# Normalising, transposing and splitting the next step's x inside the current one, and expert tiles by transposing DMAs

## The reference

```
h  = layernorm(x);  v = h@Wv+bv;  q = elu(h@Wq+bq)+1;  k = elu(h@Wk+bk)+1     # 16 heads of 16
s_t = s_(t-1) + k_t v_t^T;  z_t = z_(t-1) + k_t                               # per batch and head
x1 = x + (q_t s_t / (q_t z_t + 1e-6)) @ Wo + bo
h2 = layernorm(x1);  logits = h2 @ router_w^T;  the 2 largest of 8, softmax over them
out = x1 + sum over the 2 experts of prob * (gelu(h2 @ w1^T + b1) @ w2^T + b2)   # 256 -> 512 -> 256
```

## Time and profile before

| | us |
|---|---|
| median of 3 runs (1094.77 to 1099.10) | 1096.58 |
| profiled execution | 1091.56 |
| its span, first to last instruction | 1089.8 |
| TensorE busy | 951.3 (87%) |
| VectorE busy | 831.0 (76%) |
| ScalarE busy | 660.6 (61%) |
| GpSimd busy | 699.4 (64%) |
| xg load, issue to landing (median) | 3.0 |
| store of x1 (out<-x), issue to landing (median) | 3.2 |

### The profile page before, as it was taken

One profiled execution on the slowest core, in us unless ns is written; L12 is line 12 of the kernel. 1 busy time (PEld: TensorE's weight loads), 2 busy tenths in 40 slices (PEclk: granted clock), 3 DMA queues, 4 the chain that ended last, 5 costly groups with the idle time before them and its releaser, 6 DMA issues. The chain is left out here.

```text
span 1089.8 us, 33554 instructions
## 1 busy us (share of the span) xinstructions
PE 951.3 (87%) x10092; PEld 784.3 (72%) x10093; DVE 831.0 (76%) x2201; ACT 660.6 (61%) x1253; POOL 699.4 (64%) x606
## 2 busy tenths in 40 slices
PE   4599888988898898888889833999999999999995
PEld 2377667766766775675677733999999999999994
DVE  5378999998997997997999874666666666666663
ACT  5667776776776677666767432555555555555552
POOL 5626677786677678776778553556556565566555
PEclk9799999999998999998999966999999999999998
DMA  3665886446654654673655282455555555555554
GB/s 111 149 142 125 274 178 156 126 153 161 165 126 137 159 132 135 155 173 98 164 139 139 89 316 97 89 90 96 96 96 88 87 98 96 97 85 95 92 97 49
DMA packets 129125, 140.30 MB, mean 129 GB/s; under 512 B 12512, under 2 KB 122208, under 8 KB 128416
## 3 DMA queue, kind: packets, MB, share of 16 engines
q1 hardware_dynamic: 101184, 102.38, 38.0%
q0 software_dynamic: 26688, 35.93, 17.8%
q10 hardware_dynamic: 1184, 1.18, 0.3%
HBM read 72.01 MB, written 67.44 MB: 128 GB/s over the span
## 5 line engine op out<-in xcount | busy, mean ns | idle before, releaser
L1497 POOL DMA_INDIRECT out<-yt,to_token x142 | 225.7, 1589 | 172.8 <-DVE yt L1360 108.6
L792 ACT ACTIVATE ahl<-pS 128x512 f16<-128x512 f32 x240 | 141.0, 599 | 74.7 <-PE pS L508 73.1
L1035 DVE SCALAR_TENSOR_TENSOR ahl<-pS,ahl 128x512 f16<-128x512 f32 x240 | 161.2, 682 | 28.8 <-ACT ahl L792 27.5
L1414 POOL DMA_INDIRECT expert_in<-xn,cur x128 | 130.5, 1020 | 35.1 <-issue 33.1
L960 ACT ACTIVATE g<-pS,b1s 128x256 f32<-128x256 f32 x144 | 60.2, 470 | 90.7 <-PE pS L433 90.7
L433 PE MATMUL pF<-xT,was 128*128 128x512 f16 x384 | 102.7, 410 | 11.8 <-DVE xT L1040 11.8
L505 PE MATMUL pS<-cbs 128*128 128x512 bf16 x240 | 93.0, 387 | 20.2 <-DVE ahl L1035 12.2
L1331 DVE TENSOR_TENSOR ghl<-g,ghl 128x1024 f16<-128x1024 f32 x71 | 87.1, 1227 | 24.3 <-ACT ghl L982 24.3
L433 PE MATMUL pU<-w2s,ghl 128*128 x864 | 100.5, 273 | 1.9 <-DVE ghl L1331 1.9
L433 PE MATMUL pS<-gT,w1s 128*128 128x256 f16 x864 | 101.1, 274 | 0.1
L433 PE MATMUL pF<-w2s,ghl 128*128 x840 | 97.4, 273 | 0.0
(11 more groups left out here) (160 smaller groups left out, 2323.9 us busy)
## 6 DMA issues: line engine op xcount, KB each, us to landing
xg<-expert_in SPq DMA_DIRECT2D x71, 260.0 KB, 3.0
qk_parts<-qkhl SPq DMA_DIRECT2D x32, 512.0 KB, 2.9
qst<-qk_parts SPq DMA_DIRECT2D x96, 128.0 KB
kst<-qk_parts SPq DMA_DIRECT2D x48, 256.0 KB
xs<-x SPq DMA_DIRECT2D x16, 512.0 KB, 4.6
xr<-x SPq DMA_DIRECT2D x16, 512.0 KB, 4.8
out<-x SPq DMA_DIRECT2D x16, 512.0 KB, 3.2
expert_in<-pads SPq DMA_DIRECT2D x16, 260.0 KB, 3.7
```

What stands on the lines that cost most here:

```text
L792: nc.scalar.activation(ahl[:, b % 2, 0, n * 4 * C:(n + 1) * 4 * C], score_bank(fr, n)[:], ACT.Relu).then_inc(sc_hi, 1)
L1035: V.scalar_tensor_tensor(ahl[:, b % 2, 1, cols], score_bank(fr, n)[:], 0.0, ahl[:, b % 2, 0, cols], ALU.max, ALU.subtract).then_inc(sc_lo, 1)
L1414: G.indirect_dma_start(xg_dram, bass.IndirectOffsetOnAxis(ap=cur[:, qp, 2 * b + t:2 * b + t + 1], axis=0), xn2[:, qp, b], None).then_inc(s ...
L1497: G.indirect_dma_start(out, bass.IndirectOffsetOnAxis(ap=to_token[:, c % 2, s:s + 1], axis=0), yt[:, c % 2, s], None, compute_op=ALU.add). ...
```

## The change

1. x of step i+1: its statistics, moments and shift come early in body c, `normalise(i+1)` after the row copies' start, `x_transposes(i+1)`, `x_hi` and `x_lo` in the last third of body c. Only body 0 has them at its start, for step 0. Step 2's stand in the back-only body of step 1.
2. The order of work in a body is new on TensorE, ScalarE, VectorE and GpSimd: among others `out_transpose(r, 3)` comes after `project(1)`, `values(0)` and `values(1)` earlier, `v_low` before the third state update.
3. `norm2_apply` writes over x1 in place, after the store of x1 to the output has landed; TensorE transposes for the router from x1. New are `rows_high` (ScalarE, two per step) and `rows_low` (VectorE, two per step), which write the row as 256 f16 high parts and 256 f16 low parts in the same 1 KB that held 256 floats.
4. An expert tile comes by one DMA that transposes 256 rows x 512 f16 from DRAM into gT (128 partitions x 4 blocks x 256), and one small one for the last four floats of each row (about). There are four buffers of each in place of two; `turn`, the expert stage's `rows_high` and the low part by VectorE are gone. The loops of tiles have four tiles per turn in place of two.

```diff
+BUFS = 4
-        xn2 = sb("xn2", [P, 2, B, ROW], F32, att)
+        data = sb("data", [P, 2, B, ROW], F32, att)
-        xg = sb("xg", [P, 2, 2, ROW], F32, moe)
-        gT = sb("gT", [P, 2, 2, KC * MT], F16, moe)
+        about = sb("about", [P, BUFS, 2, ROW - D], F32, moe)
+        gT = sb("gT", [P, BUFS, 2, KC, MT], F16, moe)
+        rows = data[:].bitcast(F16)
...
@@ SP, expert tiles
-                if c >= 2:
-                    sp.wait_ge(gt_ps, t - 1)
-                    sp.wait_ge(meta, t - 1)
-                sp.dma_start(xg[:, c % 2], xg_dram[bass.ds(row, MT), :].rearrange("(s p) d -> p s d", p=P)).then_inc(xg_in[c % 2], 16)
+                if c >= BUFS or not isinstance(j, int):
+                    sp.wait_ge(h_ps, 2 * t - 2 * BUFS + 2)
+                    carry_wait(sp)
+                    sp.wait_ge(meta, t - BUFS + 1)
+                    carry_wait(sp)
+                sp.dma_start_transpose(gT[:, c % BUFS].rearrange("p a k n -> p (a k) n"),
+                                       xg_dram[bass.ds(row, MT), 0:D].bitcast(F16)).then_inc(gT_in[c % BUFS], 16)
+                sp.dma_start(about[:, c % BUFS],
+                             xg_dram[bass.ds(row, MT), D:ROW].rearrange("(s p) d -> p s d", p=P)).then_inc(about_in[c % BUFS], 16)
...
@@ TensorE, a body
-                if fr:
-                    x_transposes(0)
-                    x_transposes(1)
+                if c == 0:
+                    x_transposes(0, 0)
+                    x_transposes(0, 1)
                 if bk:
                     scores(0, 0)
-                if ro:
-                    out_transpose(r, 3)
+                if fr:
+                    project(0)
                 if bk:
                     scores(0, 1)
                 if turn_k:
                     k_rows(0)
+                if fr:
+                    project(1)
+                if ro:
+                    out_transpose(r, 3)
                 if sc:
                     route_positions()
...
-                if fr:
-                    project(0)
                 if bk:
                     scores(0, 2)
+                if turn_k:
+                    k_rows(1)
+                if fr:
+                    project(2)
                 if ro:
                     out_project(r, 3)
-                if fr:
-                    project(1)
                 if bk:
                     scores(0, 3)
-                if turn_k:
-                    k_rows(1)
-                if bk:
                     scores(1, 0)
-                if fr:
-                    project(2)
-                if bk:
                     attend(0)
+                if fr:
+                    project(3)
+                if bk:
                     scores(1, 1)
...
+                if turn_next:
+                    x_transposes(i + 1, 0)
                 if bk:
                     scores(2, 3)
                     out_project(s, 1)
+                if turn_next:
+                    x_transposes(i + 1, 1)
...
@@ TensorE, an expert tile
-                    pe.wait_ge(gt_lo, t + 2)
+                    pe.wait_ge(gT_in[p4], 16 * ((c + 1) // BUFS + 1) + 16 * j)
...
                 if is_tile(j, c + 1):
                     hidden_layer()
-                if is_tile(j, c + 2):
-                    turn()
                 if is_tile(j, c):
                     second_layer()
...
@@ ScalarE
+                def rows_high(n):
+                    act.wait_ge(xn2_done, 4 * r + 2 * n + 2)
+                    if c >= 4 and n == 0:
+                        act.wait_ge(scat_out[c % 2], 128 * rh)
+                    nc.scalar.activation(rows[:, c % 2, 2 * n:2 * n + 2, 0:D], x1[:, 2 * n:2 * n + 2], ACT.Copy).then_inc(rows_hi, 1)
...
                 if bk:
                     score_hi(0, 0)
-                if ro:
-                    out_hi(r, 3)
+                if fr:
+                    feature_in(0)
                 if bk:
                     score_hi(0, 1)
                 if turn_k:
                     kn_rows(0)
+                if fr:
+                    feature_exp(0)
+                    feature_in(1)
+                if ro:
+                    out_hi(r, 3)
...
                 if ro:
+                    rows_high(0)
                     row_copy(0)
+                    rows_high(1)
+                if turn_next:
+                    normalise(i + 1, 0)
                 if bk:
                     score_hi(2, 0)
                 if ro:
                     row_copy(1)
                 if fr:
                     qk_high(3)
+                if turn_next:
+                    normalise(i + 1, 1)
...
@@ VectorE
                 def norm2_apply(b):
                     if b == 0:
                         dve.wait_ge(ln2_rs, r + 1)
+                        dve.wait_ge(x1_out, 16 * r + 16)
-                    V.scalar_tensor_tensor(xn2[:, rp, b, 0:D], x1[:, b], mv2[:, b, 0:1], rs2[:, b:b + 1].to_broadcast([P, D]),
+                    V.scalar_tensor_tensor(x1[:, b], x1[:, b], mv2[:, b, 0:1], rs2[:, b:b + 1].to_broadcast([P, D]),
                                            ALU.subtract, ALU.mult).then_inc(xn2_done, 1)
+                def rows_low(n):
+                    dve.wait_ge(rows_hi, 2 * r + n + 1)
+                    V.scalar_tensor_tensor(rows[:, rp, 2 * n:2 * n + 2, D:2 * D], x1[:, 2 * n:2 * n + 2], 1.0,
+                                           rows[:, rp, 2 * n:2 * n + 2, 0:D], ALU.mult, ALU.subtract).then_inc(rows_lo, 1)
...
                 if bk:
                     score_lo(0, 0)
+                    score_lo(0, 1)
                 if ro:
                     out_lo(r, 3)
-                    residual(r, 2, c % 2)
-                if bk:
-                    score_lo(0, 1)
+                    residual(r, 2, c % 2, c == 2)
+                if turn_next:
+                    norm1_stats(i + 1)
                 if sc and c != STEPS:
                     row_data()
...
@@ GpSimd
                 if fr:
                     feature(0)
+                    feature(1)
+                    low(0)
                 if ro:
                     rstd(r, ve2, rs2, ln2_ve, ln2_rs)
-                if fr:
-                    feature(1)
-                    low(0)
+                if nx and c >= 2 or c == 1 and not front:
+                    rstd(i + 1, ve1, rs1, ln1_ve, ln1_rs)
+                if fr:
                     feature(2)
                     low(1)
```

More of the change, by code:

```diff
@@ L632, in body @@
                 if bk:
+                    scores(1, 1)
                     out_transpose(s, 0)
@@ L1213, in body @@
                         score_lo(1, 3)
+                    if ro:
+                        rows_low(0)
+                if fr:
+                    values(0)
                 if bk:
-                    residual(s, 0, sp_)
+                    residual(s, 0, sp_, c == 1)
+                    score_lo(2, 0)
+                if fr:
+                    values(1)
+                if bk:
+                    attention(1)
+                    state_part(1)
+                if ro and c != STEPS:
+                    rows_low(1)
                 if fr and c >= 2:
@@ L1454, in body @@
                     scatter(2)
+                if fr and c != 1 or c == 1 and not front:
+                    v_low()
                 if bk:
@@ L1458, in body @@
                     scatter(3)
-                if fr and c != 1 or c == 1 and not front:
-                    v_low()
                 if bk:
```

244 lines of the change are left out of this document (105 added, 139 removed).

## The result

The changed kernel takes 1120.25 us (1112.72 to 1123.46, 4 runs) against 1095.67 for the kernel before in the same runs: ratio 1.0212, 95% interval 1.0153 to 1.0271. It is slower by 1.5 to 2.7%; 1077 was predicted. The profiled execution took 1112.72 us (span 1110.9), 21.1 us more than the span before. It is the fastest of the four: its mean granted clock was 0.940, that of the other three 0.926 to 0.933.

What follows compares the result with a forecast made beforehand. It took TensorE to bound the expert part and VectorE the attention steps: 1091.6 - 31.2 + 11 + 0 + about 1 = 1072, plus 5.0 from profiled execution to median, gives 1077 us; 8-in-10 range 1045 to 1125.

Steps and rivals of the forecast that it cites:

- The expert part: Expert tiles: four f32 transposes leave TensorE, period 5.68 to 5.24 us, 31.2 us gained over 71 tiles, DMA just hidden.
- Rival C: Expert tiles: DMA engines become the bound and TensorE waits for gT, for example 1152 or 1230 us; chance 0.20.
- The bridge: Between attention steps and expert tiles: start -1 us, first drain step +1, filling 0; sum 0.
- so 0: In-place norm2_apply waiting for the x1 store: store needs 3 us, five VectorE instructions lie between, so no cost.
- The steps: Attention stage: a step goes from 36.8 to 37.6 us, +0.8, over 14 steps +11 us.
- about 1 for a colder TensorE at the seams: Term in the sum for TensorE's lower clock at the seams: about 1 us in the whole kernel.
- Standing that goes: VectorE standing still during GpSimd's tensor_tensor: L1136 freed, -2.0 us a step; L1119 keeps about half.
- rows_low and rows_high: Row splits added per step: two rows_high, 1.3 us on ScalarE; two rows_low, +1.2 us on VectorE, taken free of standing.
- Rival D: Attention steps eat the gain: rows_low at 1.5 us each and late k rows, steps 39.0 us, 1096 us; chance 0.19.
- out_lo late: Start of a step: VectorE idles some 1.6 + 2.0 us before out_lo(r,3), waiting for out_hi.
- score_lo(1,1) at t+18.4: Within a step, counted from the router's first instruction: score_lo(1,1) comes at t+18.4 us, today t+17.2.
- Rival B: Attention steps gain: 35.0 us each if freed VectorE time is real and out_hi not late, 1040 us; chance 0.14.

Runs made afterwards that it cites:

- e12: e6 without rows_high and rows_low, the rows sent carrying zeros for x1; 1089.75 us.
- e2: The changed kernel with the last two w2 loads and the b2 load issued after the last x1 store; 1112.19 us.
- e8: e5 with the last two w2 loads and the b2 load issued after the last x1 store; 1117.64 us.
- e11: e6 with the last two w2 loads and the b2 load issued after the last x1 store; 1073.01 us.
- e6: The changed kernel with the kernel before's order in the first part of a step; x stays early; 1078.81 us.
- e9: e6 with out_transpose, out_hi and out_lo of (r,3) put behind the second score group again; 1080.22 us.
- e3: The changed kernel with out_transpose, out_hi and out_lo of (r,3) back after the first score group; 1121.07 us.
- e15: e6 with only project(0) and project(1), and their feature_in and exp on ScalarE, two score groups earlier; 1100.63 us.
- e14: e6 with TensorE's projections early as in the changed kernel, ScalarE's order left as in e6; 1104.42 us.
- e4: The changed kernel with filler matmuls, results overwritten: eight before scores(1,0), five before attend(0); 1120.28 us.
- e7: The changed kernel without rows_high and rows_low, the rows sent carrying zeros for x1; 1174.19 us.
- e5: The changed kernel with the steps' order and x at the start as before; new expert part, split rows, in-place norm kept; 1123.40 us.

## Why the prediction was wrong

**What bounds the kernel now.** Right for the expert part. For the steps it said that VectorE paces them. With the first part in before's order the runs bear that out: taking the row splits away (e12) shortened the regular step by 1.5 us, about the 1.4 that VectorE no longer had to do, though ScalarE lost 1.3 us of work with them. In the new order it is no longer so: VectorE is idle 8.0 us of a step, and what paces the first part is the two-way chain of scores, TensorE's score, ScalarE's copy, VectorE's difference, and back to TensorE for `attend`. VectorE's 34.77 of 36.84 us hid how little slack that chain had.

**The expert part.** Mechanism and tile right: period 5.24 forecast, 5.24 measured, no wait for gT. The gain is 23.7 in place of 31.2. From the start of the first hidden layer to that of the last second layer it took 402.85 us before (1074.59 - 671.74) and 376.34 after (1092.80 - 716.46), 26.5 less, as not all tiles keep to 5.24; and what lies behind the last second layer's start grew from 15.2 to 18.1 us: GpSimd began its last scatter 11.6 us behind it (1104.40), before 8.7 (1083.32). DMA per tile: 37.5% of 5.3 is 2.0 us as forecast, and 30.2% is 1.6 us for the transposing and the small DMA together, where I had taken up to 3.1. Rival C is refuted. The small DMA's 1.1 was only ever a ceiling. The Trainium skill, "VectorE: DVE Perf Modes", section "The three transpose paths", gives 1309 ns for a 128x128 block; eight of them one after the other would be 10.5 us, an estimate, and the period of 5.24 us with no wait for gT excludes that here. What a single block takes no run shows. The Trainium skill, "DMA: Bandwidth & Descriptors", section "Latency and other measured facts", gives 261 GB/s; 256 KB in at most 1.6 us is 164 GB/s or more, which does not contradict it.

**The bridge.** Term 0, measured +3.4 (8.2 - 4.8). The start of the expert stage was better than the -1 taken (-4.8). What failed is the wait for the store of x1, put at "so 0". I had read the store's 3 us in a full step and carried it to the drain bodies, where it is queued behind four loads of w2 and one of b2. e2, e8 and e11 each took 6.6 to 7.1 us off the drain body by moving the loads; 2.1 to 5.0 of it came back as a longer way from M16 to the first hidden layer. The filling body, taken 0, cost 9.2; there VectorE waits 3.96 us for the second x, which SP issues at 115.18, behind the zeroing of the pad rows. As e6 has a long filling body too (47.9 us), the order of the first part is not its cause; I did not take it further. The last steps, M13 to M15, lost 4.6 us, of which the forecast had some 2.

**The steps.** This is the step of the prediction that failed: "So a step goes from 36.8 to 37.6, +0.8", and with it the term "about 1 for a colder TensorE at the seams". Measured in regular steps 40.4. For the eleven full steps the forecast comes to 11 x 37.6 and the 12.6 us of the loop's turns that it kept, 426.2; measured are 446.3, 20.1 more:

| | us |
|---|---|
| a step at full clock 38.8 in place of 37.6, eleven times | +13.4 |
| the first steps of a turn are no longer longer | -12.6 |
| TensorE at 1.2 GHz in ten steps, 446.3 - 11 x 38.82 | +19.3 |

The first two cancel, so the largest mis-sized term is the clock: 19 us in eleven steps where the forecast had about 1 in all. What makes it fall in that place is the new order, since e6 without that order has no such stretch in its eleven steps. The parts, one by one:

- *Standing that goes.* Right in direction: L1136 (now L1144) fell from 2.16 to 0.16 us, and VectorE's busy time by 2.4 us in spite of the two rows_low. L1119 (now L1127) went from 1.72 to 1.35, less than the half that was forecast.
- *rows_low and rows_high.* 0.68 and 0.63 us each, unhindered, as taken; their price in e6's order is 1.5 us a step (1.2 forecast). Rival D's cause is refuted; its other half, late k rows, too: TensorE waits for kst nowhere between 150 and 590 us.
- *out_lo late.* The wait came as foreseen (1.90 us). It costs nothing: e9 and e3.
- *"score_lo(1,1) at t+18.4"*, measured t+20.6 (416.00 - 395.36, the router's first instruction), and t+19.0 in the step that kept its clock. The 48 matmuls of `attend(0)` begin at t+14.6, before at t+14.2: 0.4 us later, where 0.6 was forecast (13.7 to 14.3, counted from its first matmuls). Up to there the forecast held. So 0.6 us of this part are the chain's and 1.6 the clock's, and some 0.7 more came behind score_lo(1,1), 19.9 us in place of 19.2.
- *The price of that order.* I summed the projections' 1.3 us only as a delay of `out_transpose`, and ScalarE's two features and the exponential only as a delay of `out_hi`. They also stand ahead of scores(0,1), scores(0,2) and their copies, and `attend(0)` waits behind them: its 48 matmuls begin at t+12.8 in e6, at t+14.6 in e15 and in the changed kernel. e15 measures that by itself, 1.8 us of a step with TensorE at full clock. e14 shows both engines' shares. The forecast measured itself against the kernel before, and did not see that with the early x this part could be 1.8 us shorter.
- *Cold clock, "about 1 for a colder TensorE at the seams".* In ten of eleven steps 1.4 to 2.3 us each, by the step that kept its clock, and 1.7 by e4. It falls after waits of 1.7 and 1.1 us ahead of project(3); of the ten steps with these waits one kept its clock.

With the first part's order put back the step is 37.6 us, the number forecast for the change as it stood. I take that as luck, a coincidence of two terms, since e6 has VectorE standing again (34.68 busy against 32.40).

Rival B was refuted. Rival D's 39.0 us is near the step at full clock (38.8), but by the wrong mechanism. The time lies inside the range given, at its upper end, but the sign was missed.

## What to carry to other kernels

Where three engines hand one chain to and fro (score, copy, difference, use), an instruction that is moved ahead of a link of the chain is paid by each engine in it, however idle the table of busy shares shows them; count it for every link behind it, not only for the output that one has in mind. A new wait of TensorE has a second price, the clock behind it: here ten steps had the same two waits of 1.7 and 1.1 us, nine of them were followed by 1.2 GHz, and the large group of matmuls that stood next paid for it. Price such a wait at both levels. An in-place write that waits for a store is priced by the worst place of that store in its queue, so look at the drain, where large loads are queued. And split a bundle: this one held an expert part worth 24 us, an early x with which the loop's seams were off the path in e6, a store wait of 7 us in the drain body, and an order of projections that cost more than all of it brought.

## What the runs showed of the hardware that I had not expected

- A transposing DMA of 256 rows x 512 f16 took SP 1.24 to 1.51 us to issue, median 1.26 (the small one 0.42), landed 3.4 us after its issue began (713.07 to 716.46), and raised the 16 engines' share of q1 from 1.14 us per tile (20.0% of 5.68) to 1.6, the small DMA included, while the packets of q1 went from 17205 to 92499.
- Taking work off two engines made a kernel 54 us slower (e7), with TensorE's granted clock at 0.89 for 0.94 in the window of steps.
- The same stretch of 3.4 us at 0.50 cost a step of the changed kernel 1.6 us, where project(3) and the score behind it fell into it, and a step of e11 0.2 (37.80 against 37.60), where it lay 13 to 18 us behind the step's mark.
- At the seam of a loop an engine waited with no event as the releaser: VectorE 2.4 to 2.6 us in the kernel before, 4.6 to 5.3 in e5 and 2.6 to 2.8 in e12, TensorE 3.1 to 3.3 in e4. In e6 and the changed kernel no such wait shows. What it waits for, no run shows.
